# A graph attention kernel on Trainium2: VectorE's long two-input products and subtractions cut into pieces, and one factor read from PSUM

## The reference, cut to what matters

```python
def _gat_layer(x, src, dst, edge_attr_full, W, att, b, ew, eb):
    edge_emb = edge_attr_full @ ew.T + eb
    xw = x @ W
    xj = xw[src].reshape(-1, H, D) + edge_emb.reshape(-1, H, D)
    xi = xw[dst].reshape(-1, H, D)
    att_i, att_j = (att[:, :D], att[:, D:])
    alpha = jnp.einsum('ehd,hd->eh', xi, att_i) + jnp.einsum('ehd,hd->eh', xj, att_j)
    alpha = jax.nn.leaky_relu(alpha, NEG_SLOPE)
    amax = jax.ops.segment_max(alpha, dst, num_segments=N)
    ea = jnp.exp(alpha - amax[dst])
    denom = jax.ops.segment_sum(ea, dst, num_segments=N)
    alpha = ea / (denom[dst] + EPS)
    msg = xj * alpha[..., None]
    aggr = jax.ops.segment_sum(msg, dst, num_segments=N)
    return aggr.mean(axis=1) + b
```

## Time and profile before

| | us |
|---|---|
| median of 3 runs (lowest, highest) | 3410.82 (3408.64, 3415.97) |
| the profiled execution's own time | 3413.95 |
| its span in the trace | 3412.1 |
| POOL busy (share of the span) | 2283.9 (67%) |
| DVE busy | 2095.9 (61%) |
| PE busy | 1837.5 (54%) |
| ACT busy | 676.0 (20%) |

### The profile page before, as it was taken

The page is one execution under the profiler, slowest core; times in us unless marked ns, Lnnn a source line. Parts: engine busy times, 40 slices in busy tenths (PEclk is TensorE's granted clock), DMA queues, the critical chain, the costliest instruction groups (busy, mean ns, idle before and its releaser), DMA issues.

```text
span 3412.1 us, 44842 instructions
## 1 busy us (share of the span) xinstructions
PE 1837.5 (54%) x11738; PEld 1675.8 (49%) x11738; DVE 2095.9 (61%) x6244; ACT 676.0 (20%) x3111; POOL 2283.9 (67%) x2357
## 2 busy tenths in 40 slices
PE   6879954455355455445555444554445364445436
PEld 6669943454354444445344444534445353445436
DVE  8975555665565565656655665755565584565558
ACT  0048831111114111110411111131111122111112
POOL 0047747777756777774777777477777747777773
PEclk9965565555557555555755555565555556555556
DMA  3211222222211222221122222122222212222221
GB/s 98 106 58 67 83 83 56 59 60 57 61 48 45 56 62 57 57 61 42 50 62 57 57 61 57 37 58 60 57 57 65 54 40 56 60 57 59 57 53 53
DMA packets 125699, 203.13 MB, mean 60 GB/s; under 512 B 50745, under 2 KB 88480, under 8 KB 125072
## 3 DMA queue, kind: packets, MB, share of 16 engines
q0 software_dynamic: 62560, 130.25, 15.6%
q1 hardware_dynamic: 62896, 70.01, 6.5%
HBM read 186.44 MB, written 13.68 MB: 59 GB/s over the span
## 4 chain that ended last, share of the span: by engine, by line
DVE 33%; POOL 28%; PE 18%; issue 14%; DMA 4%; DVEq 2%; ACT 1%; POOLq 0%; ACTq 0%
POOL ring L559 27%; PE bank L815 9%; DMA ring<-table,srci 3%; DVE acc L1288 2%; PE bank L857 2%; PE bank L774 2%; DVE est L1267 2%; DVE into L1226 2%; PE bank L821 2%; DVE est L1259 2%; DVE prod L1159 2%; DVE lanes L1212 2%; PE bank L812 2%; DVEq L1103 2%; DVE ring L923 2%
## 5 line engine op out<-in xcount | busy, mean ns | idle before, releaser
L559 POOL DMA_INDIRECT ring<-table,srci x1955 | 2011.6, 1029 | 632.9 <-issue 581.8
L815 PEld LDWEIGHTS bank<-pw,ring 128*128 128x128 f32 x3910 | 892.2, 330 | 28.6 <-issue 23.5
L815 PE MATMUL bank<-pw,ring 128*128 128x48 f32 x3910 | 870.3, 398 | 0.0
L812 PE MATMUL bank<-zeros 128*128 128x288 bf16 x490 | 204.0, 416 | 919.9 <-DVE pw L1244 914.2
L812 PEld LDWEIGHTS bank<-zeros 128*128 128x128 bf16 x490 | 69.8, 142 | 952.8 <-DVE pw L1244 926.8
L1188 DVE TENSOR_TENSOR alpha<-alpha,ring 128x56 f32<-128x56 f32 (+7 forms) x75 | 19.1, 254 | 842.9 <-DMA ring<-table,srci 842.7
L642 ACT ACTIVATE dd<-dd 128x66 f32<-128x66 f32 x75 | 19.4, 258 | 2232.1 <-DVE dd L1237 2232.1
L857 PE MATMUL bank<-Wl,S 128*128 128x258 f32 x250 | 151.9, 712 | 430.4 <-DVE S L1304 430.4
L1288 DVE TENSOR_TENSOR acc<-acc,bank 128x288 f32 x490 | 222.7, 454 | 181.1 <-PE bank L821 52.7
L636 ACT COPY ai_win<-ai_rows 128x48 f32 x1955 | 310.9, 228 | 57.8 <-issue 22.5
L821 PE MATMUL bank<-onehot,est 128*108 128x24 bf16 x1955 | 258.7, 246 | 85.4 <-DVE est L1268 84.9
(11 more groups left out here) (232 smaller groups left out, 2952.3 us busy)
## 6 DMA issues: line engine op xcount, KB each, us to landing
ring<-table,srci POOLq DMA_INDIRECT x1955
ai_rows<-lo_dram SPq DMA_DIRECT2D x28, 896.0 KB, 4.4
at<-in_attr SPq DMA_DIRECT2D x65, 224.0 KB, 2.6
table<-ring SPq DMA_DIRECT2D x15, 390.0 KB, 3.5
est<-in_attr_turned SPq DMA_DIRECT2D x1, 2112.0 KB, 9.9
e_dram<-ring SPq DMA_DIRECT2D x1, 1960.0 KB, 6.2
et<-e_dram SPq DMA_DIRECT2D x65, 28.0 KB
table<-ring SPq DMA_DIRECT2D x5, 325.0 KB, 3.1
```

Of the source, the lines that this page charges most:

```text
L559: nc.gpsimd.indirect_dma_start(out=ring[:, slot(t), :], out_offset=None, in_=table, in_offset=bass.IndirectOffsetOnAxis(ap=srci[:, t:t + 1 ...
L812: nc.tensor.matmul(total, zeros[:, 0:P], zeros[:, :], start=True, stop=False, skip_group_check=True)
L815: nc.tensor.matmul(wide[:, 0:H, spots[k]], ring[:, slot(t0 + k), 0:D], pw[:, g % DEEP, k, :, :], start=False, stop=False, skip_group_check ...
```

## The change

The window product is made in four pieces of tiles, the sums following one piece behind, all in part 0; part 1 keeps the addition of the edge term. The two subtractions move into `weigh` and are made per group, one on each side of the `pw` product. The probabilities are copied to PSUM bank 7 (`probs_ps`), and the product of L1259 reads them there. The semaphore `est_ready` now counts groups; SP waits for a new one, `at_used`, which is set after that product.

```diff
+WIN_PARTS = 4
...
+        probs_ps = bank[7][:, 0:H * QB].rearrange("p (h e) -> p h e", h=H)
...
-                        sp.wait_ge(est_ready, gc + 1)
+                        sp.wait_ge(at_used, gc + 1)
...
-                if t0 == TC[c]:
-                    pe.wait_ge(est_ready, layer * NC + c + 1)
+                pe.wait_ge(est_ready, gg + 1)
...
             def windows_sum(layer, c, part):
                 gc, k = layer * NC + c, CH[c]
-                ts = slice(TC[c], TC[c + 1])
                 win = ai_win[:, 0:k, :, :]
                 if part == 0:
                     v.wait_ge(win_ready, gc + 1)
-                    link(V.tensor_tensor(win, win, onehot[:, ts, :].unsqueeze(2).broadcast_to((P, k, H, WIN)), ALU.mult))
+                    cuts = [k * q // WIN_PARTS for q in range(WIN_PARTS + 1)]
+
+                    def multiply(q):
+                        a, b = cuts[q], cuts[q + 1]
+                        return mark(V.tensor_tensor(win[:, a:b], win[:, a:b],
+                                                    onehot[:, TC[c] + a:TC[c] + b, :].unsqueeze(2)
+                                                    .broadcast_to((P, b - a, H, WIN)), ALU.mult))
+
+                    def add_up(q):
+                        a, b = cuts[q], cuts[q + 1]
+                        return V.tensor_reduce(alpha[:, :, a:b].rearrange("p h k -> p k h"), win[:, a:b], AX, ALU.add)
+
+                    done = multiply(0)
+                    for q in range(WIN_PARTS):
+                        following = multiply(q + 1) if q + 1 < WIN_PARTS else 0
+                        v.wait_ge(step, done)
+                        ins = add_up(q)
+                        done = following
+                    link(ins)
+                    v.sem_inc(win_used, 1)
                 if part == 1:
-                    link(V.tensor_reduce(alpha[:, :, 0:k].rearrange("p h k -> p k h"), win, AX, ALU.add))
-                    v.sem_inc(win_used, 1)
...
             def weigh(layer, g):
                 c, t, n = GROUPS[g]
-                k = t - TC[c]
+                k = slice(t - TC[c], t - TC[c] + n)
+                whole, rest = first_part[:, c % 2, k, :], second_part[:, c % 2, k, :]
+                split = mark(V.tensor_tensor(rest, whole, first_high[:, c % 2, k, :], ALU.subtract))
                 V.tensor_tensor(pw[:, g % DEEP, 0:n, :, :],
                                 onehot[:, t:t + n, :].unsqueeze(2).broadcast_to((P, n, H, WIN)),
-                                first_part[:, c % 2, k:k + n, HF:HF + H].unsqueeze(3).broadcast_to((P, n, H, WIN)), ALU.mult)\
+                                whole[:, :, HF:HF + H].unsqueeze(3).broadcast_to((P, n, H, WIN)), ALU.mult)\
                     .then_inc(p_ready, 1)
+                v.wait_ge(step, split)
+                V.tensor_tensor(third_part[:, c % 2, k, :], rest, second_high[:, c % 2, k, :], ALU.subtract)\
+                    .then_inc(est_ready, 1)
...
             def chain_probs(layer, c):
...
-                pr = probs[:, :, 0:k].rearrange("p h k -> p k h")
-                done = mark(V.tensor_copy(es[:, :, HF:HF + H], pr))
+                V.tensor_copy(es[:, :, HF:HF + H], probs[:, :, 0:k].rearrange("p h k -> p k h"))
+                link(V.tensor_copy(probs_ps, probs[:, :, :]))
                 V.tensor_tensor(es[:, :, HF + H:EC], maxes[:, :, 0:k].rearrange("p h k -> p k h"),
                                 last_col[:, TC[c]:TC[c + 1]].unsqueeze(2).broadcast_to((P, k, H)), ALU.mult)
-                whole = mark(V.tensor_tensor(es[:, :, 0:HF].rearrange("p k (h f) -> p k h f", h=H),
-                                             at[:, gc % NAT, 0:k, :].unsqueeze(2).broadcast_to((P, k, H, FA)),
-                                             pr.unsqueeze(3).broadcast_to((P, k, H, FA)), ALU.mult))
-                v.wait_ge(step, done)
+                link(V.tensor_tensor(es[:, :, 0:HF].rearrange("p k (h f) -> p k h f", h=H),
+                                     at[:, gc % NAT, 0:k, :].unsqueeze(2).broadcast_to((P, k, H, FA)),
+                                     probs_ps[:, :, 0:k].rearrange("p h k -> p k h").unsqueeze(3)
+                                     .broadcast_to((P, k, H, FA)), ALU.mult))
+                v.sem_inc(at_used, 1)
                 for g in GC[c][0:2 if c else AHEAD]:
                     weigh(layer, g)
-                v.wait_ge(step, whole)
-                rest, last = second_part[:, c % 2, 0:k, :], third_part[:, c % 2, 0:k, :]
-                link(V.tensor_tensor(rest, es, first_high[:, c % 2, 0:k, :], ALU.subtract))
-                V.tensor_tensor(last, rest, second_high[:, c % 2, 0:k, :], ALU.subtract).then_inc(est_ready, 1)
```

More of the change, by code:

```diff
@@ L367, in program @@
         est_ready = sem("est_ready")
+        at_used = sem("at_used")
         acc_zero = sem("acc_zero")
```

## The result

| | before | changed |
|---|---|---|
| median of all runs, us (lowest, highest) | 3412.47 (3408.64, 3415.97), 4 runs | 3312.9 (3312.0, 3313.11), 4 runs |
| profiled execution; its span | 3413.95; 3412.1 | 3313.11; 3311.3 |
| DVE busy in the span, instructions | 2095.9, 6244 | 2204.8, 7599 |
| POOL busy in the span | 2283.9 | 2157.9 |

The ratio of changed to before is 0.9708 (95% interval 0.9691 to 0.9725): 99.6 us faster, with 109 us more work on DVE. The forecast was 3331 us, 80 us faster, with a range from 3302 to 3380.

What follows compares the result with a forecast made beforehand. The row gathers' pitch, lengthened by DVE operations with two SBUF inputs, bounds the kernel. Span 3412.1 - 91.5 (surplus) + 11.5 (layers' ends) = 3332.1; as a median 3410.8 - 80 = 3331 us, range 3302 to 3380.

Steps and rivals of the forecast that it cites:

- What bounds: First gather to chunk 12's landing: time is gathers times pitch; two-SBUF-input DVE operations hold gathers, surplus 153.9 us.
- DVE's added work: Steady part: about 1.5 us more DVE work per chunk, covered by its 13.0 us wait for rows.
- The product frees the gather: Product of L1259: with probabilities in PSUM its 0.61 us hold becomes 0; copy 0.24 us, product stays 1.35 us.
- The surplus after: Gathers up to chunk 12: 1.0 us lost per chunk instead of 2.3, saving 91.5 us in five layers.
- the 0.127 us: Gather's age at the one moment when it waits for the end of the two-SBUF-input DVE operation then running.
- The range's lower bound: Surplus 0.65 us per chunk and layer's end 0 to 1 us: 3300 by its sum, stated as 3302.
- The layer's end: From chunk 12's landing to the node update: +2.3 us a layer, +11.5 in five; bounds 0 to 5 a layer.
- The waits that move: PE waits per group, SP's attribute loads wait for the product: nothing late, no time gained or lost.
- The PSUM operand: Rival: a PSUM input doesn't free the product, 37 to 56 us of gain lost, about 3377 us; chance 0.07.
- "something else" rival: Gathers' surplus isn't due to two-input operations and stays 30.8 us a layer: 3422 us, slower; chance 0.03.
- The first, at 0.05: Rival: a run of pieces holds a gather as one operation, so splitting gives nothing back: 3494 us; chance 0.05.
- that sign of the prediction: Changed trace: no gather above about 1.5 us.

Runs made afterwards that it cites:

- added_two_sbuf: Changed kernel plus three useless 896-column operations with two SBUF inputs each, before the scan of chunks 1 to 12 of each layer: 3359.0 us.
- late_chunks_old: Changed kernel with DVE's work after chunk 12's landing in the old form (whole operations, product from SBUF, weights not waiting for the product): 3298.8 us, ratio 0.9664.
- product_from_sbuf: Changed kernel with the product of the edge terms reading its probabilities from SBUF again, the copy to PSUM kept: 3357.4 us, ratio 0.9837.

## Why the prediction was right, step by step

- **What bounds.** Right: the gathers' pitch, and their surplus. DVE's added work, about 1.5 us a chunk, took 13.0 us of waiting to 9.7 together with the 1.8 us by which the landings of two chunks came nearer (117.7 / 65). (The terms listed for the 1.5 add up to 1.3; DVE's busy time grew by 109 us, 1.7 a chunk.) The runs with added operations show the cover by themselves.
- **The product frees the gather.** Right, and the product's speed stayed (1.34 us for 1.35). The copy to PSUM takes 0.22 us, and the next operation starts 0.26 us after it does; 0.24 was expected.
- **The surplus after.** Mechanism right, size off: 12.5 us a layer forecast, 7.6 measured (38.0 / 5), 117.7 us saved over the stretches for 91.5. This term is 26 us off and the layers' ends are 5 us off the other way; together they make the 20 us between the 80 forecast and the 99.6 measured. The numbers of moments were met: 264 gathers had theirs in a group's piece (4.1 x 65 = 267), 83 in a window piece (1.3 x 65 = 85). What was too large is the loss at each: 0.085 us for my 0.17, and 0.19 for my 0.25. I had let a piece hold over its whole recorded length. In the traces it holds 0.1 to 0.15 us less: in the changed kernel all 65 gathers with a moment 0.08 to 0.155 us after the start of a group's piece lost nothing. (Earlier moments fall into the end of the operation before.) Of a piece of 0.35 us about 0.2 then hold, and half of that is 0.1. In added_two_sbuf the border lies elsewhere: 19 of the 21 moments at 0.104 to 0.119 us were held to the operation's end. Since the 0.127 us are themselves inferred from the ends, the traces show that the hold is shorter than the record, and not at which edge. (The range's lower bound comes to 3300 by its own sum, not 3302, which changes nothing here.)
- **The layer's end.** 2.3 us a layer forecast, 3.3 measured, 3.5 in the first layer, which the following parts are from. The last part came as worked out: from chunk 14's first weights to the node update 7.67 us before and 7.03 after, -0.64, TensorE's groups following at 2.14 us. Before it, DVE's time grew by 2.0 us up to chunk 13's scan (1.3 forecast), by 1.3 up to chunk 14's (1.0) and by 0.8 to the weights (0.6). One group follows another after 0.79 us, not 0.76, and behind a group an add's base load lies bare by about 0.1 us each time; I had counted that once per chunk. late_chunks_old, which undoes only DVE's part, takes the growth back, so it is DVE's.
- **The waits that move.** Right: TensorE's waits of 85 us for L1268 are gone, POOL never waits beyond 0.3 us for the ring, and SP's wait for attributes costs nobody anything.
- **The rivals.** The PSUM operand and the "something else" rival are out (product_from_sbuf, added_two_sbuf). The first, at 0.05, is wrong for this change in its size, 3313 us and not 3494 (its own terms add up to 3493). But its mechanism occurs. The prediction said that a gather waits for the end of the operation then running and no longer, and that none would take over about 1.5 us. In the changed kernel 8 gathers of the stretches take 1.50 to 2.34 us and lose 6.5 us together. The longest:

```profile
1094.80 0.35 DVE L1264 TENSOR_TENSOR est<-est 128x144 f32<-128x144 f32 x1
1094.96 2.34 POOL L563 DMA_INDIRECT ring<-table,srci  x1 [0.30 <-issue]
...
1096.13 0.35 DVE L1270 TENSOR_TENSOR est<-est 128x144 f32<-128x144 f32 x1
1096.39 0.20 DVE L1294 TENSOR_SCALAR dd<-phi_mask,dd 128x1 f32<-128x1 f32 x1
```

Its moment, 1095.09, lies in L1264, and it ends at 1097.30, 0.82 us after the L1270 that ends at 1096.48: it sat through six pieces. So "no longer" is false, and that sign of the prediction failed. The cost stayed small, because this happened 8 times in 1820; nothing in the prediction assured that. One cut further on it costs 33 us.

## What to carry to other kernels

Where a stream of indirect DMAs issued by GpSimd sets the pace, look at the length of single issues, not at their number: a long one ends a fixed time after a VectorE operation, and that names the operation. Put one input of it in PSUM first (44.5 us here, for a copy of 0.22 us), cut the rest into pieces of a third to half a microsecond, with one-input work in between where the order allows it, and stop there: finer window pieces gained nothing, and groups in pieces of 0.25 us without a break cost 33 us. Cut only where somebody waits for the stream: the old form behind the last awaited landing gave 14 us back.

## What the runs showed of the hardware that I had not expected

- The hold is 0.1 to 0.15 us shorter than the operation's record, so pieces of 0.35 us cost a gather half of what their length suggests (0.085 us on average for 0.17).
- Back-to-back two-input operations of 0.25 us hold a gather across several of them (up to over 0.4 us, 51 gathers); in the changed kernel, with such operations of 0.35 us, 8 of 1820 gathers lost as much. Where a sum, an add from PSUM or a scalar operation followed the piece, a waiting gather always went on (99 of 99).
- An fp32 copy of 448 columns takes 0.38 us at the least and holds gathers like an operation with two SBUF inputs, up to its end.
- The beat between the gathers and one chunk's pieces moved 8 to 16 us from one line to another in the three runs that undo a part. That is more than the finer window pieces were worth, which was nothing.
